# Two-layer attention block with FiLM: a permuted order of calls at the layer change

## The chip, the cores and the metric

One core of one Trainium2 chip runs the kernel. The metric is the device time of one execution in microseconds, from the first to the last work of the core; lower is better. Three runs of the kernel before are shown, and one more execution was recorded by the profiler.

## The reference, cut to what matters

The input x has 32 tiles of 128 tokens by 512 features. Two layers run over each tile, with the weights and masks of their own; a third input, cond, gives a scale and a shift per tile (FiLM).

```python
def layer(x, cond, mask, heads):            # heads: 16 in layer 0, 8 in layer 1
    xn = layernorm(x) * norm_scale + norm_bias
    q, k, v = xn @ Wq + bq, xn @ Wk + bk, xn @ Wv + bv
    k, v = masked(k, mask), masked(v, mask)
    q = softmax(q, over the features of a head)
    k = softmax(k, over the tokens)
    att = k.T @ v                           # per head
    y = q @ att
    scale, shift = split(silu(cond) @ film_W + film_b)
    h = silu(layernorm(y) * (1 + scale) + shift)
    return x + h @ Wo + bo
x = layer(x, cond, mask0, 16); x = layer(x, cond, mask1, 8)
```

All is float32. Each of the four large products is made as three products of split operands (high part times high part, high times low, low times high).

## The kernel before, in words

**Tiles and steps.** A tile is one batch entry (128 x 512). Tiles 0 to 31 belong to layer 0, tiles 32 to 63 are the same rows of X again in layer 1, and step s computes the keys, values and queries of tile s. The kernel is a software pipeline over 64 steps, written out by hand: each engine has a block with a list of calls, and in the steady part one function `step(s)` that lists the calls of one step. Engines meet only at semaphores: a call waits for the counts of its inputs and of the readers of what it overwrites, and raises a count of its own. There is no planner at run time; the order of the calls on each engine is the order of the work. An engine that waits lets nothing of its list pass.

**What a tile goes through.** Tiles of x are turned in pairs g (tiles 2g and 2g+1). VectorE: `stat_x` (mean and variance), GpSimd: `root_x`, ScalarE: `norm_x`, VectorE: `turn_x` (transpose in blocks of 32 by 32), SyncE: `write_x`, `read_x` (through a buffer in HBM, which finishes the transpose), ScalarE: `x_turned` (scale and bias, and the high part XH), GpSimd: `x_low` (the low part XL). TensorE: `keys` (24 matmuls of 256 columns), `values` and `queries` (12 matmuls of 512 columns each). The keys go on by VectorE `keys` (mask, maximum), ScalarE `exp_k`, VectorE `key_sums`, GpSimd `normalise_keys`, VectorE `turn_keys`, and in pairs by SyncE `write_keys` and `place_keys` into EK. The values go by VectorE `values` and ScalarE `values`. The queries go by VectorE `queries`, GpSimd `queries`, VectorE `turn_queries`, then SyncE `write_qy` and `read_qy` into QT, and ScalarE `exp_q`. TensorE: `attention(j)` (32 small matmuls on EK and VV), ScalarE: `heads(j)` (copies the result to ATT), TensorE: `mix(j)` (8 matmuls on EQ and ATT). Then VectorE `mixed`, GpSimd `root_y`, ScalarE `norm_y`, VectorE `turn_y`, again `write_qy` and `read_qy` (q of tile s-1 and y of tile s-3 travel in one transfer, so `exp_q(j)` needs `read_qy(j+1)` and `film(o)` needs `read_qy(o+3)`), ScalarE `film` (four pieces and a tanh), VectorE `h_mul`, ScalarE `h_high`, GpSimd `h_low`, TensorE `output` (12 matmuls of 512 columns), VectorE `add_x`. GpSimd's `add_bo` adds the output bias to X ahead of that.

**Lines.** `split_low` is at 308, `load_second` at 316, the calls of SyncE at 362 to 431, of GpSimd at 573 to 645, of ScalarE at 768 to 893, of TensorE at 1081 to 1205 (all matmuls of the large products have line 1091, attention 1171, mix 1187), of VectorE at 1394 to 1561.

**Buffers that bind the order.** XS, QS, QT, XT, KT, EK, XF0, H, HH and HL exist once; XH, XL, SK and the HBM buffers twice; VV three times. PSUM has one bank each for keys, values, queries and outputs, so `keys(i)` on TensorE waits for VectorE's `keys(i-1)`, and likewise for the others; `attention(j)` waits for `heads(j-1)`:

```python
eng.wait_ge(ld_ek[g % 2], placed(g))   # attention(j), g = j // 2
eng.wait_ge(act_v, j + 1)
eng.wait_ge(act_att, j)
eng.wait_ge(pe_att, j + 1)             # heads(j)
eng.wait_ge(pe_y, j)
```

**The layer change.** Steps 31 to 36 are written out separately on every engine (SyncE 500 to 541, GpSimd 699 to 748, ScalarE 977 to 1046, TensorE 1318 to 1353, VectorE 1737 to 1820), because the four weights of layer 1 come in there. Weight w (4 to 7: k, v, q, o) is loaded into the one buffer STAGE in four chunks by `load_second(eng, w, [c])`, each of which waits until the same chunk of weight w-1 has been split. ScalarE's `split_high(w, [c])` makes the high part and waits until the last product of layer 0 with the old weight is done; VectorE or GpSimd makes the low part by `split_low(eng, w, [c])`. The first product of layer 1 with a weight waits for its chunks one by one:

```python
for c in range(C):
    if fresh is not None:
        eng.wait_ge(low_w[fresh][c], 1)
```

The calls of `load_second_bias` fetch the three bias rows of layer 1. The film weights are loaded in halves behind `write_qy` in even steps up to 20, in `step` of SyncE.

Of the kernel before, what the change touches and what calls it, by code (L numbers as in the profile page):

```python
# [44 lines left out]
def build_blocks(nc, x, cond, mask0, mask1, weights, film_w, vec_rows, bias_rows, out):  # L45
# [21 lines left out]
    with ctx:  # L67
# [273 lines left out]
        def _(eng):  # L341
# [160 lines left out]
            write_qy(31)  # L502
            load_second(eng, 5, [1])
            load_second(eng, 5, [0])
            load_second(eng, 5, [2])
            load_second(eng, 5, [3])
            read_qy(31)
            read_x(17)
            write_keys(15)
            load_second_bias(0, dve_v)  # L510
            load_second(eng, 6, [0])
            load_second(eng, 6, [1])
            load_second(eng, 6, [2])
            load_second(eng, 6, [3])
            place_keys(15)
            load_second_bias(1, dve_q)
            write_qy(32)
            read_qy(32)
            masks_at(32)
            write_keys(16)  # L520
            write_qy(33)
            read_qy(33)
            place_keys(16)
            write_x(18)
            read_x(18)
            write_qy(34)
            read_qy(34)
            masks_at(34)
            load_second(eng, 7, [0])
            load_second(eng, 7, [1])  # L530
            load_second(eng, 7, [2])
            load_second(eng, 7, [3])
            write_x(19)
            write_qy(35)
            read_x(19)
            read_qy(35)
            write_keys(17)
# [18 lines left out]
        def _(eng):  # L556
# [143 lines left out]
            root_y(28)  # L700
            split_low(eng, 4, [1])
            h_low(27)
            x_low(33)
            normalise_keys(31)
            root_x(36)
            mask_of_keys(16)
            queries(31)
            root_y(29)
            h_low(28)
            split_low(eng, 6, [1])  # L710
            split_low(eng, 6, [3])
            x_low(34)
            normalise_keys(32)
            root_x(37)
            normalise_keys(33)
            queries(32)
            root_y(30)
            h_low(29)
            x_low(35)
            root_x(38)  # L720
            mask_of_keys(17)
            queries(33)
            add_bo(32)
            add_bo(33)
            add_bo(34)
            root_y(31)
            h_low(30)
            x_low(36)
            normalise_keys(34)
            root_x(39)  # L730
            queries(34)
            add_bo(35)
            root_y(32)
            h_low(31)
            x_low(37)
            normalise_keys(35)
            root_x(40)
            mask_of_keys(18)
            queries(35)
            add_bo(36)  # L740
            root_y(33)
            split_low(eng, 7, [1])
            split_low(eng, 7, [3])
            h_low(32)
            x_low(38)
            normalise_keys(36)
            root_x(41)
            queries(36)
# [18 lines left out]
        def _(eng):  # L767
# [210 lines left out]
            film(27)  # L978
            norm_y(28)
            exp_q(29)  # L980
            split_high(4, [0])
            split_high(4, [1])
            h_high(27)
            split_high(4, [2])
            split_high(4, [3])
            x_turned(33)
            exp_k(31)
            heads(29)
            split_high(5, [0])
            split_high(5, [1])  # L990
            split_high(5, [2])
            split_high(5, [3])
            film(28)
            values(31)
            h_high(28)
            norm_y(29)
            split_high(6, [0])
            split_high(6, [1])
            split_high(6, [2])
            split_high(6, [3])  # L1000
            exp_q(30)
            norm_x(36)
            x_turned(34)
            exp_k(32)
            heads(30)
            values(32)
            exp_k(33)
            film(29)
            h_high(29)
            norm_y(30)  # L1010
            exp_q(31)
            x_turned(35)
            heads(31)
            norm_x(37)
            values(33)
            film(30)
            h_high(30)
            norm_x(38)
            norm_y(31)
            x_turned(36)  # L1020
            exp_k(34)
            exp_q(32)
            heads(32)
            values(34)
            norm_x(39)
            film(31)
            norm_y(32)
            x_turned(37)
            h_high(31)
            exp_k(35)  # L1030
            exp_q(33)
            heads(33)
            values(35)
            split_high(7, [0])
            split_high(7, [1])
            split_high(7, [2])
            split_high(7, [3])
            norm_x(40)
            film(32)
            norm_y(33)  # L1040
            x_turned(38)
            h_high(32)
            exp_k(36)
            exp_q(34)
            heads(34)
# [31 lines left out]
        def _(eng):  # L1077
# [254 lines left out]
            queries(33)  # L1332
            attention(31)
            output(29)
            mix(31)
            keys(34)
            values(34)
            queries(34)
# [9 lines left out]
            keys(36)  # L1348
            values(36)
            queries(36)  # L1350
# [544 lines left out]
```

## Time and profile before

| what | value |
|---|---|
| median of three runs | 878.02 us (877.77 to 879.38) |
| profiled execution | 877.97 us, span of its instructions 876.2 us |
| mean granted clock of TensorE | 0.994 |
| busy in the span: TensorE, VectorE, ScalarE, GpSimd | 843.5, 679.9, 607.6, 549.5 us |
| transfers | 169.81 MB, 194 GB/s over the span |
| chain that ended last | TensorE 84%, DMA 6%, VectorE 4% |

The span runs from the first to the last instruction; the execution's own time has 1.8 us more around it. All times in the views below are counted from the start of the span. Busy time of TensorE counts matmuls whatever their clock, so a slow clock hides in it; the granted clock stands beside it as a share of full speed.

### The profile page before, as it was taken

What the parts mean: (1) busy time and instruction counts of PE and PEld (TensorE: products, weight loads), DVE (VectorE), ACT (ScalarE), POOL (GpSimd) and SP (SyncE); (2) the same over time, 40 slices, a digit from 0 to 9 for tenths busy, and PEclk for the clock granted to TensorE, in tenths of its full rate; (3) what the DMA queues carried; (4) which work ended last, traced back from release to release, by engine and by line L of the source; (5) the groups of instructions that cost most, each with busy time, mean ns of one, the idle gap of its engine ahead of it and who ended that gap; (6) DMA issues with size and microseconds to landing.
All of it is one profiled execution on the core that took longest, in us unless ns stands there. A gap on an engine that the chain in (4) does not pass through costs nothing.

```text
span 876.2 us, 19904 instructions
## 1 busy us (share of the span) xinstructions
PE 843.5 (96%) x6581; PEld 715.2 (82%) x6581; DVE 679.9 (78%) x1352; ACT 607.6 (69%) x1441; POOL 549.5 (63%) x741
## 2 busy tenths in 40 slices
PE   4989999999999999999978999999999999999997
PEld 4768888888888888888867888888888888888885
DVE  5987777778778778877977887787788788777765
ACT  5566777676777677677775866776776777677564
POOL 2475765765766766676657667667656766765541
PEclk9999999999999999999999999999999999999999
DMA  9875766776766665556754656556666655656431
GB/s 315 292 205 172 221 206 188 223 213 196 222 199 204 205 216 186 167 176 192 211 175 151 217 174 200 183 182 196 186 193 199 200 177 178 195 192 198 150 134 61
DMA packets 115549, 169.81 MB, mean 194 GB/s; under 512 B 11871, under 2 KB 84695, under 8 KB 115447
## 3 DMA queue, kind: packets, MB, share of 16 engines
q1 hardware_dynamic: 114656, 167.56, 60.9%
q8 instruction: 53, 0.87, 0.4%
q10 hardware_dynamic: 790, 0.98, 0.4%
q14 instruction: 50, 0.40, 0.2%
HBM read 95.61 MB, written 72.88 MB: 192 GB/s over the span
## 4 chain that ended last, share of the span: by engine, by line
PE 84%; DMA 6%; DVE 4%; issue 2%; ACT 2%; SPq 2%; POOL 0%; ACTq 0%; DVEq 0%
PE PS L1091 74%; PE PS L1187 6%; PE PS L1171 3%; DMA QT<-qy_turned 1%; DMA x_turned<-XS 1%; DMA X<-in_x 1%; DMA qy_turned<-QS 1%; SPq L405 1%; DMA k_turned<-KT 0%; PE PS L1233 0%; SPq L420 0%; DVE WL_k L313 0%; DMA EK<-k_turned 0%; DMA XT<-x_turned 0%; SPq L380 0%
## 5 line engine op out<-in xcount | busy, mean ns | idle before, releaser
L635 POOL TENSOR_TENSOR HL<-H,HH 128x512 fp32r<-128x512 f32 x60 | 78.3, 1305 | 186.6 <-ACT HH L855 186.4
L822 ACT ACTIVATE Z<-QT,FC,FA 128x128 f32<-128x128 f32 x240 | 99.1, 484 | 100.4 <-DMA QT<-qy_turned 100.4
L1091 PE MATMUL PS<-XH,WH_k 128*128 128x256 f32 x512 | 152.0, 297 | 2.6 <-DVE XL L1448 2.5
L1091 PE MATMUL PS<-XH,WL_k 128*128 128x256 f32 x512 | 146.5, 286 | 0.0
L1091 PE MATMUL PS<-XL,WH_k 128*128 128x256 f32 x512 | 146.5, 286 | 0.0
L1091 PE MATMUL PS<-WH_o,HH 128*128 128x512 f32 x248 | 104.2, 420 | 6.6 <-issue 6.4
L892 ACT ACTIVATE XN<-X,NBX,RSX 128x512 f32<-128x512 f32 x60 | 48.8, 813 | 79.2 <-POOL NBX L584 79.2
L1091 PEld LDWEIGHTS PS<-XH,WH_k 128*128 128x128 f32 x512 | 99.9, 195 | 4.2 <-issue 4.1
L784 ACT ACTIVATE SK<-SK,KN 128x128 f32<-128x128 f32 x256 | 98.9, 387 | 5.9 <-DVE KN L1466 5.9
L1091 PE MATMUL PS<-WH_q,XH 128*128 128x512 f32 x256 | 101.4, 396 | 0.3 <-DVE SQ L1493 0.3
L1091 PE MATMUL PS<-WH_v,XH 128*128 128x512 f32 x256 | 100.6, 393 | 0.0
L1091 PE MATMUL PS<-WL_q,XH 128*128 128x512 f32 x256 | 100.4, 392 | 0.0
L1091 PE MATMUL PS<-WL_v,XH 128*128 128x512 f32 x256 | 100.3, 392 | 0.0
L1091 PE MATMUL PS<-WH_q,XL 128*128 128x512 f32 x256 | 100.2, 391 | 0.0
L1091 PEld LDWEIGHTS PS<-XL,WH_k 128*128 128x128 f32 x512 | 100.0, 195 | 0.0
L1091 PEld LDWEIGHTS PS<-XH,WL_k 128*128 128x128 f32 x512 | 99.7, 195 | 0.0
L1091 PE MATMUL PS<-WH_v,XL 128*128 128x512 f32 x256 | 99.6, 389 | 0.0
L1091 PE MATMUL PS<-WL_o,HH 128*128 128x512 f32 x248 | 98.1, 396 | 0.0
L1091 PE MATMUL PS<-WH_o,HL 128*128 128x512 f32 x248 | 98.0, 395 | 0.0
L622 POOL TENSOR_TENSOR XL<-XF,XH 128x512 fp32r<-128x512 f32 x60 | 77.7, 1295 | 9.1 <-ACT XH L881 8.9
L606 POOL TENSOR_TENSOR X<-X,BB 128x512 f32<-128x512 f32 x64 | 82.8, 1296 | 0.4
L1561 DVE TENSOR_TENSOR X<-PS,X 128x512 f32<-128x512 f32 x64 | 44.2, 690 | 46.0 <-PE PS L1091 45.9
(155 smaller groups left out, 2111.4 us busy)
## 6 DMA issues: line engine op xcount, KB each, us to landing
qy_turned<-QS SPq DMA_DIRECT2D x60, 512.0 KB, 2.9
QT<-qy_turned SPq DMA_DIRECT2D x240, 128.0 KB, 3.0
k_turned<-KT SPq DMA_DIRECT2D x32, 512.0 KB, 4.1
EK<-k_turned SPq DMA_DIRECT2D x128, 128.0 KB, 2.8
x_turned<-XS SPq DMA_DIRECT2D x30, 512.0 KB, 2.8
XT<-x_turned SPq DMA_DIRECT2D x120, 128.0 KB, 3.5
out_x<-X SPq DMA_DIRECT2D x32, 256.0 KB, 3.4
X<-in_x SPq DMA_DIRECT2D x11, 512.0 KB, 4.9
```

The lines of the kernel that those rows point to most:

```text
L405: eng.dma_start(QT[32 * fq:32 * fq + 32, :, 0:n, :, :].rearrange("p q h c n -> p q (h c n)"), src[fq])\
L606: eng.tensor_tensor(X[:, b, :], X[:, b, :], BB[:, 2, :], ALU.add).then_inc(pool_bo, 1)
L622: eng.tensor_tensor(XL[g % 2][:, dst, :], XF0[:, :, :], XH[g % 2][:, dst, :].bitcast(F32), ALU.subtract).then_inc(pool_xl, 1)
L635: eng.tensor_tensor(hl_of(o), h_of(o), hh_of(o).bitcast(F32), ALU.subtract).then_inc(pool_hl, 1)
L784: e = eng.activation(SK[:, p, a, :], SK[:, p, a, :], ACT.Exp, bias=KN[:, p, t, cc:cc + 1], accum_out=SE[:, p, a:a + 1])
L822: z = eng.activation(z_of(o)[:, c * P:c * P + P].rearrange("p (q n) -> p q n", q=Q), src, ACT.Identity, bias=FC[l][:, c, b:b + 1], scale=F ...
L892: eng.activation(XN[:, t, :], X[:, n % B, :], ACT.Identity, bias=NBX[:, r:r + 1], scale=RSX[:, r:r + 1]).then_inc(act_xn, 1)
L1091: mm = eng.matmul(dst, left[a](c), right[b](c), start=(c == 0 and a + b == 0), stop=(c == C - 1 and a == 1))
L1171: mm = eng.matmul(PS[f:f + 32, B_ATT, c * P + a:c * P + a + w], vs if l == 0 else ks, ks if l == 0 else vs, start=True, stop=True, tile_po ...
L1187: mm = eng.matmul(bank(B_Y + c // 2, (c % 2) * W, W), EQ[:, c * P:c * P + P], ATT[:, c // 2, (c % 2) * W:(c % 2 + 1) * W], start=True, sto ...
L1561: eng.tensor_tensor(X[:, b, :], PS[:, bank_out(o), :], X[:, b, :], ALU.add).then_inc(dve_x, 1)
```

## The change

Only the order of calls in steps 31 to 36 changes, on all five engines. Every list holds the same calls before and after, so each instruction and each transfer is issued once as before, with the same waits and sizes. Out of their places move 22 calls of TensorE's list, 73 of VectorE's, 64 of ScalarE's, 40 of GpSimd's and 34 of SyncE's (counted as positions at which the lists differ). The loading of the film halves is in the steady steps and is left as it is. On TensorE:

```diff
@@ -1318,36 +1318,36 @@
 keys(31)
 values(31)
 queries(31)
+keys(32)
 attention(29)
+keys(33)
+mix(29)
 output(27)
-mix(29)
-keys(32)
-keys(33)
 values(32)
 output(28)
 attention(30)
+attention(31)
+mix(30)
 queries(32)
-mix(30)
 values(33)
 queries(33)
-attention(31)
-output(29)
 mix(31)
 keys(34)
+queries(34)
 values(34)
-queries(34)
 attention(32)
+output(29)
+mix(32)
+queries(35)
 output(30)
-mix(32)
 keys(35)
+attention(33)
 values(35)
-queries(35)
-attention(33)
 output(31)
 mix(33)
 keys(36)
+queries(36)
 values(36)
-queries(36)
 attention(34)
 output(32)
 mix(34)
```

On the other engines the order after the change is this (the order before is in the functions above, at the lines named).

SyncE, lines 500 to 541:

```python
load_second(eng,5,[0]); load_second(eng,5,[1]); load_second(eng,5,[2]); write_qy(31); load_second(eng,5,[3]);
load_second(eng,6,[0]); read_qy(31); write_keys(15); load_second(eng,6,[1]); write_x(17);
load_second(eng,6,[2]); place_keys(15); load_second_bias(0, dve_v); load_second_bias(1, dve_q);
load_second(eng,6,[3]); load_second_bias(2, pool_bo); read_x(17); write_qy(32); read_qy(32); masks_at(32);
load_second(eng,7,[0]); write_keys(16); write_qy(33); masks_at(34); load_second(eng,7,[1]); read_qy(33);
place_keys(16); write_qy(34); write_x(18); read_qy(34); load_second(eng,7,[2]); load_second(eng,7,[3]);
read_x(18); write_qy(35); read_qy(35); write_x(19); write_keys(17); read_x(19); place_keys(17); write_qy(36);
read_qy(36); masks_at(36)
```

GpSimd, lines 699 to 748:

```python
add_bo(31); root_y(28); root_x(36); split_low(eng,4,[1]); x_low(33); normalise_keys(31); mask_of_keys(16);
queries(31); h_low(27); h_low(28); root_y(29); normalise_keys(32); root_x(37); split_low(eng,6,[1]);
split_low(eng,6,[3]); normalise_keys(33); root_y(30); x_low(34); queries(32); add_bo(32); x_low(35);
root_x(38); root_x(39); mask_of_keys(17); root_x(40); root_y(31); queries(33); h_low(29); add_bo(33);
add_bo(34); add_bo(35); queries(34); h_low(30); root_y(32); add_bo(36); h_low(31); x_low(36);
normalise_keys(34); x_low(37); mask_of_keys(18); normalise_keys(35); queries(35); root_y(33); h_low(32);
split_low(eng,7,[1]); root_x(41); split_low(eng,7,[3]); normalise_keys(36); queries(36); x_low(38)
```

ScalarE, lines 977 to 1046:

```python
norm_x(35); x_turned(33); split_high(4,[0]); split_high(4,[1]); norm_y(28); split_high(4,[2]);
split_high(4,[3]); film(27); split_high(5,[0]); exp_k(31); exp_q(29); values(31); h_high(27);
split_high(5,[1]); split_high(5,[2]); heads(29); split_high(5,[3]); split_high(6,[0]); film(28); exp_q(30);
h_high(28); exp_k(32); exp_k(33); split_high(6,[1]); norm_y(29); heads(30); split_high(6,[2]);
split_high(6,[3]); heads(31); x_turned(34); values(32); x_turned(35); norm_y(30); exp_q(31); norm_x(36);
film(29); norm_x(37); norm_y(31); h_high(29); exp_q(32); film(30); norm_x(38); heads(32); norm_x(39);
h_high(30); values(33); exp_k(34); film(31); exp_q(33); norm_y(32); h_high(31); x_turned(36); x_turned(37);
exp_k(35); heads(33); split_high(7,[0]); norm_x(40); split_high(7,[1]); split_high(7,[2]); film(32);
exp_q(34); norm_y(33); h_high(32); values(34); split_high(7,[3]); exp_k(36); heads(34); x_turned(38);
values(35); values(36)
```

VectorE, lines 1737 to 1820:

```python
stat_x(36); mixed(28); stat_x(37); stat_x(38); turn_queries(30); split_low(eng,4,[0]); turn_x(35); turn_y(28);
split_low(eng,4,[2]); keys(31); split_low(eng,4,[3]); values(31); split_low(eng,5,[0]); h_mul(27);
key_sums(31); add_x(26); queries(31); split_low(eng,5,[1]); turn_keys(31); keys(32); split_low(eng,5,[2]);
split_low(eng,5,[3]); mixed(29); h_mul(28); add_x(27); keys(33); key_sums(32); split_low(eng,6,[0]);
stat_x(39); stat_x(40); key_sums(33); turn_queries(31); turn_y(29); split_low(eng,6,[2]); mixed(30);
values(32); queries(32); turn_keys(32); turn_keys(33); turn_queries(32); turn_y(30); add_x(28); values(33);
mixed(31); queries(33); h_mul(29); turn_x(36); second_ones(); keys(34); turn_queries(33); turn_y(31);
queries(34); turn_x(37); h_mul(30); add_x(29); mixed(32); turn_x(38); turn_x(39); key_sums(34);
turn_queries(34); h_mul(31); turn_y(32); add_x(30); values(34); queries(35); keys(35); values(35); stat_x(41);
key_sums(35); turn_keys(34); turn_keys(35); mixed(33); add_x(31); split_low(eng,7,[2]); turn_queries(35);
h_mul(32); split_low(eng,7,[0]); turn_y(33); keys(36); queries(36); turn_x(40); key_sums(36); values(36);
turn_keys(36)
```

## Rows read from the trace of the kernel before

**Rows 1.** The page: busy time and share of the span of each engine

```profile
PE 843.5 (96%) x6581; PEld 715.2 (82%) x6581; DVE 679.9 (78%) x1352; ACT 607.6 (69%) x1441; POOL 549.5 (63%) x741
```

**Rows 2.** Windows: length, busy us by engine, granted clock, DMA share, GB/s

```profile
400.00:450.00 50.00, 45.62 (x368) 38.80 (x368) 41.30 (x74) 36.03 (x82) 33.20 (x41) 0.97 0.72 208
450.00:500.00 50.00, 45.68 (x330) 38.85 (x330) 38.53 (x76) 34.59 (x80) 34.25 (x45) 0.97 0.55 175
...
700.00:800.00 100.00, 99.97 (x782) 85.13 (x781) 78.64 (x156) 73.04 (x175) 65.61 (x88) 1.00 0.58 188
...
445.00:450.00 5.00, 4.51 (x43) 3.63 (x44) 2.48 (x7) 4.08 (x14) 2.92 (x4) 0.66 0.43 139
```

**Rows 3.** The chain, 400 to 540: start us, us, what (mix 27, 28, 34, 35)

```profile
403.40 0.90 PE PS L1187 x8
...
416.02 0.91 PE PS L1187 x8
...
505.80 0.90 PE PS L1187 x8
...
518.62 0.90 PE PS L1187 x8
```

**Rows 4.** Timeline of TensorE: start, us, line, tiles, shape, count, idle before and releaser

```profile
425.18 0.46 PE L1171 MATMUL PS<-EK,VV 128*32 128x32 f32 x32
...
439.78 0.47 PE L1091 MATMUL PS<-WH_o,HH 128*128 128x512 f32 x1 [1.44 <-issue]
...
445.49 0.46 PE L1171 MATMUL PS<-EK,VV 128*32 128x32 f32 x32 [2.67 <-DMA EK<-k_turned]
...
450.33 1.06 PE L1187 MATMUL PS<-ATT,EQ 128*128 128x132 f32 x8
...
477.48 2.10 PE L1187 MATMUL PS<-ATT,EQ 128*128 128x132 f32 x8 [3.22 <-ACT EQ L802]
```

**Rows 5.** Timeline of SyncE's queue, the issue of place_keys(15)

```profile
437.40 1.75 SPq L420 DMA_DIRECT2D EK<-k_turned  x4
```

**Rows 6.** The chain, 400 to 540: transfers of the q and y rounds

```profile
440.60 6.44 DMA qy_turned<-QS
...
448.37 4.24 DMA QT<-qy_turned
...
457.86 2.59 DMA qy_turned<-QS
```

**Rows 7.** Timeline of ScalarE: heads(29), and the first piece of x_turned(36)

```profile
427.29 0.57 ACT L841 ACTIVATE ATT<-PS 128x512 f32<-128x512 f32 x1
...
473.09 1.10 ACT L874 ACTIVATE XF<-XT,VC 128x256 f32<-128x256 f32 x2 [2.05 <-DMA XT<-x_turned]
```

**Rows 8.** VectorE's groups, 415 to 510: shapes, count | busy us, mean ns | idle before

```profile
L313 DVE TENSOR_TENSOR WL_k<-STAGE,WH_k 128x512 fp32r<-128x512 f32 x3 | 5.1, 1764 | 0.0
...
L1400 DVE BATCH_NORM_STATS2 BNX<-X 128x6 f32<-128x512 f32 x6 | 4.1, 678 | 0.0
...
L1464 DVE TENSOR_TENSOR KB<-KM,VC 128x4 f32<-128x4 f32 x6 | 3.1, 521 | 0.2
...
L313 DVE TENSOR_TENSOR WL_q<-STAGE,WH_q 128x512 fp32r<-128x512 f32 x2 | 1.3, 671 | 1.5 <-ACT WH_q L774 1.5
```

**Rows 9.** Timeline of VectorE: turn_x(35), keys(31), h_mul(27); mixed(29), h_mul(28)

```profile
418.80 0.68 DVE L1422 STREAM_TRANSPOSE XS<-XN 128x512 f32<-128x512 f32 x1
...
420.00 0.65 DVE L1460 TENSOR_TENSOR SK<-PS,MB 128x512 f32<-128x512 f32 x1
...
421.69 0.68 DVE L1547 SCALAR_TENSOR_TENSOR H<-H,Z 128x512 f32<-128x512 f32 x1
...
434.73 0.24 DVE L1527 RECIPROCAL RQ<-PS 128x16 f32<-128x16 f32 x1
...
436.56 0.66 DVE L1547 SCALAR_TENSOR_TENSOR H<-H,Z 128x512 f32<-128x512 f32 x1
```

**Rows 10.** The page: GpSimd's h_low, mean ns of one

```profile
L635 POOL TENSOR_TENSOR HL<-H,HH 128x512 fp32r<-128x512 f32 x60 | 78.3, 1305 | 186.6 <-ACT HH L855 186.4
```

More of the change, by code:

```diff
@@ L499, in _ @@
                 step(s)
-            write_x(17)
-            load_second_bias(2, pool_bo)
[L502 to L507, printed above, removed]
-            read_x(17)
[L509 to L516, printed above, removed]
+            load_second(eng, 5, [0])
+            load_second(eng, 5, [1])
+            load_second(eng, 5, [2])
+            write_qy(31)
+            load_second(eng, 5, [3])
+            load_second(eng, 6, [0])
+            read_qy(31)
+            write_keys(15)
+            load_second(eng, 6, [1])
+            write_x(17)
+            load_second(eng, 6, [2])
+            place_keys(15)
+            load_second_bias(0, dve_v)
+            load_second_bias(1, dve_q)
+            load_second(eng, 6, [3])
+            load_second_bias(2, pool_bo)
+            read_x(17)
             write_qy(32)
@@ L977, in _ @@
             norm_x(35)
-            film(27)
-            norm_y(28)
-            exp_q(29)
+            x_turned(33)
             split_high(4, [0])
             split_high(4, [1])
-            h_high(27)
+            norm_y(28)
             split_high(4, [2])
             split_high(4, [3])
-            x_turned(33)
+            film(27)
+            split_high(5, [0])
             exp_k(31)
-            heads(29)
-            split_high(5, [0])
+            exp_q(29)
+            values(31)
@@ L990, in _ @@
+            h_high(27)
             split_high(5, [1])
             split_high(5, [2])
+            heads(29)
             split_high(5, [3])
+            split_high(6, [0])
             film(28)
-            values(31)
+            exp_q(30)
             h_high(28)
+            exp_k(32)
+            exp_k(33)
+            split_high(6, [1])
             norm_y(29)
-            split_high(6, [0])
-            split_high(6, [1])
+            heads(30)
             split_high(6, [2])
             split_high(6, [3])
-            exp_q(30)
@@ L1002, in _ @@
-            norm_x(36)
+            heads(31)
             x_turned(34)
-            exp_k(32)
-            heads(30)
             values(32)
-            exp_k(33)
-            film(29)
-            h_high(29)
+            x_turned(35)
             norm_y(30)
             exp_q(31)
-            x_turned(35)
-            heads(31)
+            norm_x(36)
+            film(29)
             norm_x(37)
-            values(33)
[L1016 to L1019, printed above, removed]
@@ L1020, in _ @@
-            x_turned(36)
[L1021 to L1027, printed above, removed]
+            norm_y(31)
+            h_high(29)
+            exp_q(32)
+            film(30)
+            norm_x(38)
+            heads(32)
+            norm_x(39)
+            h_high(30)
+            values(33)
+            exp_k(34)
+            film(31)
+            exp_q(33)
+            norm_y(32)
+            h_high(31)
@@ L1028, in _ @@
+            x_turned(36)
             x_turned(37)
-            h_high(31)
             exp_k(35)
-            exp_q(33)
             heads(33)
-            values(35)
             split_high(7, [0])
+            norm_x(40)
             split_high(7, [1])
             split_high(7, [2])
+            film(32)
+            exp_q(34)
+            norm_y(33)
+            h_high(32)
+            values(34)
             split_high(7, [3])
-            norm_x(40)
-            film(32)
-            norm_y(33)
+            exp_k(36)
@@ L1041, in _ @@
+            heads(34)
             x_turned(38)
[L1042 to L1045, printed above, removed]
+            values(35)
             values(36)
```

158 lines of the change are left out of this document (79 added, 79 removed).

## Prediction, made before the changed kernel was seen to run

> **What bounds the kernel now.** I began with the page: TensorE is busy in 843.5 of 876.2 us, no other engine in more than 680 [rows 1]. So TensorE is the bound, and what can be won is its idle time. The windows say where that lies: in 100 us late in layer 1 it is busy 99.97 us, but at the layer change it misses 4.38 us of 400 to 450 and 4.32 of 450 to 500 [rows 2]. In one of these stretches the granted clock is 0.66 (between the levels 1.2 and 2.4 GHz), so some time is lost while TensorE counts as busy [rows 2].
>
> The whole price comes from the chain, which passes through every mix. Two mixes of layer 0 lie 416.02 - 403.40 = 12.62 us apart, two of layer 1 518.62 - 505.80 = 12.82 [rows 3]. From mix(28) at 416.02 to mix(34) at 505.80 there are six steps, three with attention of each layer: 3 x 12.62 + 3 x 12.82 = 76.3 us if nothing waits. They take 89.8. **13.5 us** is the most that this change can give.
>
> The timeline of TensorE and the chain's transfers tell who takes them. Output(28) comes after 1.44 us of idle; attention(30) after 2.67, waiting for EK [rows 4]. Then from attention(30) at 445.49 to mix(30) at 450.33 pass 4.84 us where a full clock needs 3.2: 1.6 us to the clock, after a stretch with two holes. Mix(32) waits 3.22 us for exp_q(32), and its eight matmuls take 2.10 us, against some 0.9 in the chain of other steps [rows 3, 4]. The rest, 13.5 - 1.4 - 2.7 - 1.6 - 3.2 - 1.2 = 3.4, is in short holes and the slow matmuls behind mix(32). Why EK is late: place_keys(15) is issued at 437.40 behind four weight chunks, and attention(30) starts 8.1 us later [rows 5]. The write of QS at 440.60 takes 6.44 us to land, a like one at 457.86 takes 2.59; its read takes 4.24 [rows 6]. Why exp_q(32) is late: on ScalarE it stands behind x_turned(36) and exp_k(34), and x_turned(36) starts only at 473.09, after 2.05 us of waiting for read_x(18) [rows 7], which exp_q(32) has no need of.
>
> **The change, engine by engine.** It adds and removes no instruction and no transfer: each engine issues the same calls in another order, with the same waits. Direct cost zero; the price is in who waits for whom. I walked the new order by hand with durations of the trace, from 416.02, where both kernels are still alike.
>
> *Weight splits and keys(32).* New: keys(32) stands directly behind queries(31), free at 425.18 [rows 4], instead of behind attention, output and mix. It needs the split chunks of weight 4 and VectorE's keys(31). The first of the two transposes ahead of VectorE's keys(31) began at 418.80, right behind mixed(28), and keys(31) itself at 420.00, so a transpose is worth 0.6. From 418.8 the new order has two stat_x (0.68 and an aggregate: 0.8 each), three transposes (turn_queries, turn_x, turn_y: 0.62 each), two splits (0.65 each) and keys(31), which takes 421.69 - 420.00 = 1.69 [rows 8, 9]: 1.6 + 1.9 + 1.3 + 1.7 = 6.5, thus 425.3. Split 4[3] follows at 425.9 and is needed only by the last quarter of a product. One collision with GpSimd (below) would add 1.1. Loss: between 0.1 and 1.3, I take **0.7**, the middle, since one of the two splits faces GpSimd's own.
>
> *Keys(33), mix(29), output(27).* Keys(33) covers heads(29), which is good. Output(27) needs h_low(27), now behind root_x(36), the split, x_low(33), normalise_keys(31), the mask and queries(31) on GpSimd: my walk has it 0.1 us after mix(29). Between 0 and one h_low of 1.3 [rows 10]; I take **0.1**, as all that stands before it was ready early.
>
> *Output(28).* Film(28) needs read_qy(31), which SyncE may issue only after split 4[3], split 5[0] and exp_q(29); h_mul(28) waits on VectorE for mixed(29) behind four splits; then h_high and h_low. TensorE has values(32) to do meanwhile. Between 0 and the present 1.44; **0.5** by the walk.
>
> *Attention(30), attention(31), mix(30).* Place_keys(15) now has only two chunks and a write ahead of it instead of four chunks, and its keys are turned at about 431.3. A write of 4 us and a placing of 5, between the transfers of [rows 6], put EK at 440 to 441, and attention(30) wants it at 441.6. But attention(31) now stands directly behind attention(30) and needs heads(30), which reads what attention(30) wrote: a bubble of 0.57 [rows 7] and two handovers, **0.7**, that the old order did not have. In return attention(31) need not be fetched in later.
>
> *Queries(32), values(33).* Values(33) needs values(32) of VectorE, behind split 6[2] and mixed(30) (436.56 - 434.73 = 1.83 [rows 9]): **0.3**, between 0 and 1.1.
>
> *Steps 34 to 36.* Queries(34) goes ahead of values(34), output(29) goes behind attention(32), output(30) behind queries(35). So h_low(29) and h_low(30) gain three to six us of cover. On ScalarE, exp_q(32) stands ahead of both x_turned(36) and exp_k(34), so the 3.22 us wait and its slow clock go. Exp_q(33) and exp_q(34) come 7 us or more ahead of their mixes. Cost 0 in the walk. This cover is work of TensorE itself; without it the 3.22 would be back. What is late next are places with less than 0.8 us to spare: exp_q(31) for mix(31) (0.5), x_low(35) for keys(34) (0.7), EK for attention(32) and (34) (0.5 each), h_low(29) and (30) (0.6, 0.8), split 7[3] for output(32) (0.3). For these seven I add **2.0**, between 0 and 7 x 0.6 = 4.2; nearest to the low end, since a slip shifts all later work on other engines too and a second place pays only the difference.
>
> *The queues.* SyncE's waits are strict: write_qy(33) now waits behind write_keys(16) and a chunk of weight 7; read_qy(34) behind write_x(18), which waits for turn_x(37). Both are in the walk; the latter's cover is 4 us. Masks_at(34) and two chunks of weight 7 move up, to the calm behind step 32. GpSimd comes out of step 36 some 4 us later relative to mix(34) than now (x_low(38) behind mix(34), not ahead of it), and keys(38) wants x_low(39) 3 us after it can be ready: hidden. The film halves are loaded in earlier steps, unchanged.
>
> **Sum.** 0.7 + 0.1 + 0.5 + 0.7 + 0.3 + 2.0 = 4.3 us lost of 13.5: a gain of 9.2. The profiled execution took 877.97 (span 876.2 and 1.8 around it), so 868.8; the median, 878.02, stands 0.05 above it, which I neglect. After step 36 TensorE is saturated, so a gain there stays a gain at the end. From the ends of the terms: lost 0 + 0.1 + 0 + 0.7 + 0 + 0 to 1.3 + 1.3 + 1.4 + 0.7 + 1.1 + 4.2, or 0.8 to 10.0, times of 865.3 to 874.5, all at one end only together.
>
> **One row against the change: the collisions.** A split of weight 4 on VectorE takes 1764 ns, one of weight 6 takes 671; the sum KB, with both inputs in SBUF, four elements wide, takes 521 on average [rows 8]. The long ones ran while GpSimd worked on wide tiles. The Trainium skill (SBUF — State Buffer, section Who interferes with whom) says that a VectorE operation with two SBUF inputs and a GpSimd operation that reads SBUF lock each other out for a whole instruction. The trace agrees for the splits of weight 4. The new order packs splits, h_mul and keys on VectorE against h_low, mask and queries on GpSimd between 421 and 437, where TensorE hangs on VectorE.
>
> **The rivals.** *A, collisions everywhere.* The five splits that gate (4[0], 4[2], 5[1] to 5[3]) each lose 1764 - 671 = 1.1: 5.5 us in place of the 0.7 and some of the thin places: 868.8 + 5.5 - 1.7 = **872.6**. For: the three of weight 4 all lost it. Against: those of weight 5 did not, on average. 0.17.
> *B, transfers as crowded as now, and the clock with them.* EK takes 8.1 us from its issue again [rows 5]: issued about 435.5, it lands at 443.6, 2.0 after attention(30) wants it, and the clock falls again for 1.6: 868.8 + 3.6 = **872.4**. Against: two of the four chunks now come after it. 0.12. The Trainium skill (TensorE: Matmul & The Clock Gate, HAM oscillation) says too that waits for DMA take the clock down; the trace agrees at 445 to 450 [rows 2], and rival B has its price from rows.
> *C, slower: the round of q and y becomes the bound.* Rounds 31, 32 and 33 (write, read, then exp_q and film) each gate TensorE with at most 1.0, 0.5 and 0.6 us to spare. If each write takes 6.44 instead of 2.59 [rows 6], 3 x 3.85 - 2.1 = 9.5 are lost beside the 2.3 of the sum's first terms and 3.2 of clock: 15.0 against 13.5, **879.5**. It decides from about 3.4 us of excess (13.5 - 2.3 - 3.2 + 2.1, by three) in each of the three. Against: only one write in this stretch took that long, and the crowd of chunks ahead of it is spread now. 0.07.
> *D, nothing gained: the idle time only moves.* GpSimd's lag of 4 us after step 36, if its slack of 3 is not there, makes each following step wait until the old phase is restored: up to the whole 9.2, **878**. Against: GpSimd is busy in 549.5 of 876.2 us [rows 1]. 0.05.
> The forecast itself: 0.59.
>
> **How the numbers follow.** Likeliest: 868.8. The range 865.8 to 873.9 takes in the forecast's bounds nearly whole and A and B with a us of excess; outside are C, D and the far ends of the others, under 0.2. A measurement of this kernel can tell 0.2% (1.8 us) from no change. Faster by more: forecast, A and B, 0.88. Within: D, 0.05. Slower: C, 0.07.
>
> **What would show it.** The windows 400 to 450 and 450 to 500 should show TensorE busy 47 to 49 us each, with no granted clock under 0.9 in any 5 us. Mix(34) should come near 496.6. The waits of TensorE should name no EQ, and EK for under 1 us. ScalarE should do exp_q(32) ahead of x_turned(36). Right for A: splits of weights 4 and 5 with a mean over 1200 ns. Wrong altogether: a wait of over 2 us on QT or EK, or one on XL after 500.

## The result, and the profile after

| | before | after |
|---|---|---|
| median of 6 runs each, same chip | 878.31 us (877.55 to 881.51) | 872.59 us (871.42 to 874.24) |
| ratio, 95% interval | | 0.9927 (0.9911 to 0.9944) |
| profiled execution, span | 877.97, 876.2 us | 871.58, 869.8 us |
| mean granted clock | 0.994 | 0.994 |

The change makes the kernel 5.7 us faster, where 9.2 were forecast. The page's busy line of after answers to [rows 1]: each engine is busy for as long as before, within 3 us, in a shorter span.

```profile
PE 843.4 (97%) x6581; PEld 715.4 (82%) x6581; DVE 677.0 (78%) x1352; ACT 606.4 (70%) x1441; POOL 548.5 (63%) x741
```

The windows of after, with the columns of [rows 2]:

```profile
400.00:450.00 50.00, 48.33 (x419) 40.85 (x419) 43.43 (x88) 38.29 (x93) 35.39 (x47) 1.00 0.69 207
450.00:500.00 50.00, 48.00 (x340) 40.58 (x339) 39.42 (x75) 36.38 (x83) 37.02 (x46) 0.97 0.67 205
...
465.00:470.00 5.00, 4.42 (x43) 3.55 (x44) 1.50 (x3) 3.07 (x6) 4.16 (x4) 0.72 0.83 284
```

TensorE has gained 2.71 and 2.32 us of busy time in the two stretches of the layer change. One slow stretch is left, now at 465 to 470. The chain of after, 400 to 540 (start us, us, what), gives the price by the mixes of [rows 3] (mix 28 and 34):

```profile
417.13 0.91 PE PS L1187 x8
...
454.30 3.48 DMA qy_turned<-QS
...
461.79 3.75 DMA EK<-k_turned
465.58 0.65 PE PS L1171 x32
...
499.28 0.90 PE PS L1187 x8
```

From mix(28) at 417.13 to mix(34) at 499.28 pass 82.15 us. Before it was 89.8, and 76.3 without any wait. So 5.8 us are still lost, and 7.6 of 13.5 are won. The waits of TensorE from 400 to 540 (releaser: us in total, times, longest us) say where they are:

```profile
PE PS L1171 <- DMA EK<-k_turned: 2.0, 1, 2.0
PE PS L1171 <- ACT ATT L841: 0.9, 1, 0.9
PE PS L1091 <- DVE KN L1466: 0.7, 1, 0.7
```

The wait on EQ of [rows 4] is gone. The timeline of TensorE shows the same three idle times at keys(32), attention(31) and attention(32), and a fourth loss that no wait shows:

```profile
427.12 0.35 PE L1091 MATMUL PS<-XH,WH_k 128*128 128x256 f32 x1 [0.75 <-DVE KN L1466]
...
444.38 0.46 PE L1171 MATMUL PS<-EK,VV 128*32 128x32 f32 x32 [0.93 <-ACT ATT L841]
...
465.58 0.65 PE L1171 MATMUL PS<-VV,EK 128*32 128x64 f32 x32 [2.00 <-DMA EK<-k_turned]
...
466.51 0.39 PE L1091 MATMUL PS<-WL_o,HH 128*128 128x512 f32 x1
...
468.07 0.63 PE L1091 MATMUL PS<-WH_o,HH 128*128 128x512 f32 x1
...
470.61 1.06 PE L1187 MATMUL PS<-ATT,EQ 128*128 128x132 f32 x8
```

Inside output(29) a matmul takes first 0.39 and then 0.63 us: the clock has gone down behind the hole, toward the lower of its two levels (0.72 of 2.4 GHz over the 5 us). From attention(32) at 465.58 to mix(32) at 470.61 pass 5.03 us. A variant shown below (the round of y earlier) has the same calls there at a full clock: 465.50 to 468.99, 3.49 us. The clock cost 1.5.

At attention(30), where before waited 2.67 us for EK, TensorE's matmuls show no wait. But it was close. The weight load ahead of its matmuls (engine PEld) still waits:

```profile
442.99 0.35 PEld L1171 LDWEIGHTS PS<-EK,VV 128*32 128x32 f32 x32 [0.37 <-DMA EK<-k_turned]
```

Place_keys(15) was issued at 436.38, 6.6 us ahead of that.

Why EK is late stands in the timeline of SyncE (start and length of the issue):

```profile
451.79 0.43 SPq L411 DMA_DIRECT2D k_turned<-KT  x1
454.30 0.33 SPq L390 DMA_DIRECT2D qy_turned<-QS  x1
...
457.80 2.53 SPq L405 DMA_DIRECT2D QT<-qy_turned  x4
460.42 1.80 SPq L420 DMA_DIRECT2D EK<-k_turned  x4
```

The keys that place_keys(16) fetches were written by the issue of 451.79, and that write landed 4.7 us later, near 456.5. But place_keys(16) stands behind read_qy(33), which waits for write_qy(33), issued at 454.30 and landed at 457.78 (the chain's 3.48 us). So place_keys(16) goes out at 460.42, lands at 465.54, and attention(32) starts at 465.58. Write_qy(33) in turn waits for turn_y(30) (453.51), which ScalarE's norm_y(30) sets (452.68). That stands in line behind x_turned(35) (451.02), which waits for GpSimd's x_low(34) (449.62 to 450.92). Two things end just ahead of x_low(34): x_turned(34) of ScalarE (447.50 to 449.25) and GpSimd's own root_y(30) (to 449.53), which stands ahead of it in the list. X_turned(34) waited for read_x(17), issued at 440.15 and landed at 447.48, 7.3 us later.

### The profile page after: what moved, and what is told of

It reads as the page before. It is cut to its first block, busy times and chain, and to the rows that moved or that the text cites. A ratio compares the mean times of both kernels' runs of the same rounds, so it can differ in the third digit from the quotient of the medians.

```text
span 869.8 us, 19904 instructions
## 1 busy us (share of the span) xinstructions
PE 843.4 (97%) x6581; PEld 715.4 (82%) x6581; DVE 677.0 (78%) x1352; ACT 606.4 (70%) x1441; POOL 548.5 (63%) x741
## 4 chain that ended last, share of the span: by engine, by line
PE 81%; DMA 8%; DVE 3%; ACT 2%; SPq 2%; issue 2%; POOL 1%; DVEq 0%; ACTq 0%; POOLq 0%
PE PS L1091 71%; PE PS L1187 6%; PE PS L1171 3%; DMA X<-in_x 2%; DMA QT<-qy_turned 2%; DMA k_turned<-KT 2%; SPq L405 1%; DMA qy_turned<-QS 1%; DMA EK<-k_turned 1%; DMA XT<-x_turned 1%; SPq L420 1%; ACT XF L874 1%; PE PS L1233 0%; PE PS L1243 0%; ACT YN L791 0%
```

## The experiments

Below, "28 to 34" is the time from mix(28) to mix(34) in the profiled execution (89.8 before, 82.15 after). The ratio is always to the kernel before on the same chip. Three chips were used for the experiments: the first for the repeat and the next three runs (before had a median of 878.92 us there), the second for weight 7 late, the stat_x, the round of y and the three mends together (880.10), the third for the last four (879.65). The changed kernel was run again on the first alone, so a later order is compared with it across chips. Between the times of two executions there is a shift as well: mix(28) begins at 415.0 to 417.4 over the 14 traces of this study. And from mix(34) to mix(58) they take 307.7 to 309.6 us, so that a difference of a us between 28 and 34 need not show in the median.

**The same kernel again,** without any edit, on the chip of the next three.

> The changed kernel once more, beside the other orders of this call. 872.6 by its runs so far; all theories expect 871.5 to 874, with attention(32) some 2 us late on EK and a slow output(29) behind it.

It took 871.16 us, 0.9921 (0.9902 to 0.9939) of before, with 82.9 us from mix(28) to mix(34). The wait on EK is 1.8 us, the clock from 465 to 470 is 0.73. The size of the gain and both halves of the loss at attention(32) are the kernel's and not one execution's.

**Place_keys(16) ahead of read_qy(33)** on SyncE.

```diff
-read_qy(33)
 place_keys(16)
+read_qy(33)
```

> SyncE issues place_keys(16) ahead of read_qy(33) instead of behind it. Theory 1 (the queue's own order: the keys landed in HBM at 456.5 but place_keys(16) was issued at 460.4, behind the wait for the write of q and y): EK lands near 461.5, the wait of attention(32) (2.0) and the slow clock behind it (1.6) go, 3.6 us less than the changed kernel, about 869.0. Theory 2 (the transfers are crowded, so EK lands late wherever it is issued): within 1 us of the changed kernel. Theory 3 (collisions of VectorE and GpSimd took the gain): no change.

871.94 us, 0.9927 (0.9910 to 0.9944), 28 to 34 82.4 us; the 869.0 of the first theory did not come. The timeline of SyncE, and then those of TensorE and ScalarE:

```profile
457.06 1.75 SPq L420 DMA_DIRECT2D EK<-k_turned  x4
458.92 2.72 SPq L405 DMA_DIRECT2D QT<-qy_turned  x4
```

```profile
454.48 1.17 PE L1187 MATMUL PS<-ATT,EQ 128*128 128x132 f32 x8 [1.09 <-ACT EQ L802]
...
463.95 0.65 PE L1171 MATMUL PS<-VV,EK 128*32 128x64 f32 x32
...
469.35 1.14 PE L1187 MATMUL PS<-ATT,EQ 128*128 128x132 f32 x8 [1.75 <-issue]
```

```profile
465.23 0.63 ACT L802 ACTIVATE EQ<-QT 128x512 f32<-128x512 f32 x1 [3.25 <-DMA QT<-qy_turned]
```

Attention(32) no longer waits, and the clock stays full. So the place of the loss is right: the queue's order made EK late. But the time is the same. The read of q and y is now issued 1.1 us later, ScalarE waits 3.25 us for it, exp_q(32), film(30) and heads(32) follow late, and mix(32) waits 1.75 us. Mix(31) loses another 1.09. Which of two transfers goes first moves the wait; both cannot be early in a queue with that much ahead of them.

**Chunk 3 of weight 6 and read_x(17) ahead of the three bias rows,** to take away the first cause of the late norm_y(30).

```diff
 place_keys(15)
+load_second(eng, 6, [3])
+read_x(17)
 load_second_bias(0, dve_v)
 load_second_bias(1, dve_q)
-load_second(eng, 6, [3])
 load_second_bias(2, pool_bo)
-read_x(17)
```

> Weight chunk 6[3] and read_x(17) go ahead of the three bias rows. Theory 1 with its root one step earlier (x_turned(34) waits for read_x(17), so norm_y(30), turn_y(30), write_qy(33), read_qy(33) and place_keys(16) are all late): x_turned(34) starts 1 to 2 us earlier and place_keys(16) with it, so the wait for EK halves: 1 to 3 us less than the changed kernel. If read_x(17) is only one of several equals, under 0.5.

872.15 us, 0.9921 (0.9897 to 0.9946); 28 to 34 81.2 us. The read landed near 445.7 and x_turned(34) began at 446.29, 1.2 us earlier than in after. The wait on EK stayed at 1.89. X_low(34) came only 0.2 us earlier, as GpSimd does it behind its own root_y(30); its timeline:

```profile
449.06 0.27 POOL L594 TENSOR_SCALAR NBY<-MVY,RSY 128x1 f32<-128x1 f32 x1
449.41 1.30 POOL L622 TENSOR_TENSOR XL<-XF,XH 128x512 fp32r<-128x512 f32 x1
```

So x_turned(35) (450.81) and norm_y(30) (452.47) were 0.2 us earlier too, and no more. That cause, taken alone, is refuted. The clock stayed full behind this hole, which is about what 28 to 34 is shorter (0.9 to 1.7 us). The median does not show it: from mix(34) to mix(58) this execution took 309.63 us, 1.7 more than after.

**SyncE's list as in before,** with the new order on the four other engines (its 34 places, listed ahead of the prediction, go back to the order of before).

> SyncE's order of before, the other engines as in the changed kernel. Theory 1: the order of the queue matters a lot; place_keys(16) stands behind read_qy(33) here too and masks_at(34) and weight 7 come later: 0 to 3 us slower than the changed kernel. Theory 2 (crowding): the chunks of weight 6 are again all ahead of place_keys(15), EK is late for attention(30) as in the kernel before, 2 to 4 us slower, near 875. If the gain was all in the compute engines: within 1 us of the changed kernel.

891.06 us, 1.0142 (1.0121 to 1.0163); 28 to 34 102.1 us. Waits of TensorE, 400 to 540:

```profile
PE PS L1091 <- POOL HL L635: 7.0, 1, 7.0
PE PS L1091 <- DVE VV L1505: 6.9, 1, 6.9
PE PS L1187 <- issue: 3.7, 1, 3.7
```

None of the theories allowed for that much: the worst had 2 to 4 us more than after, and it is 20. The orders of the five engines belong together. With SyncE's left behind, the same change costs 12 us instead of giving 6. The releasers named are compute engines, though only the order of transfers differs from after: they are late themselves. Part of the loss is the clock, 0.51 from 450 to 455 and 0.50 from 495 to 500, behind the two holes of 7 us.

**Place_keys(16) ahead, and two chunks of weight 7 and masks_at(34) behind read_qy(34).**

```diff
-load_second(eng, 7, [0])
 write_keys(16)
 write_qy(33)
-masks_at(34)
-load_second(eng, 7, [1])
-read_qy(33)
 place_keys(16)
+read_qy(33)
 write_qy(34)
 write_x(18)
 read_qy(34)
+masks_at(34)
+load_second(eng, 7, [0])
+load_second(eng, 7, [1])
 load_second(eng, 7, [2])
```

> Place_keys(16) ahead of read_qy(33) as before, and masks_at(34) with weight chunks 7[0] and 7[1] moved back behind read_qy(34). With place_keys(16) alone ahead, the wait went from EK at attention(32) to EQ at mix(31) and mix(32). If those are late because the transfers of steps 32 and 33 are crowded by the chunks and the mask (theory 2), read_qy(33) lands 2 us or more earlier, mix(32) does not wait, and the time is 868.5 to 870. If it is the chain of q and y before the write that is late (theory 1b), read_qy(33) lands within 1 us of where it did and the time stays at 871 to 872.

875.83 us, 0.9951 (0.9933 to 0.9968); 28 to 34 85.1 us. Timeline of ScalarE, then of TensorE:

```profile
480.54 1.09 ACT L874 ACTIVATE XF<-XT,VC 128x256 f32<-128x256 f32 x2 [2.90 <-DMA XT<-x_turned]
```

```profile
487.64 1.14 PE L1187 MATMUL PS<-ATT,EQ 128*128 128x132 f32 x8 [2.74 <-issue]
```

Up to mix(32) the order does what it was meant to: that mix no longer waits and comes 51.9 us after mix(28), against 53.8 with place_keys(16) ahead alone. But all four chunks now stand in one block ahead of read_x(18), which lands near 480.5. X_turned(36) waits for it, and behind that stand heads(33) and film(32). Mix(33) waits 2.74 us. The chunks have to go somewhere; ahead of read_x(18) is the wrong place.

**The four stat_x of the change put later** on VectorE: 37 and 38 where 39 and 40 stood, 39 behind turn_keys(33), 40 behind h_mul(29).

```diff
-stat_x(37)
-stat_x(38)
 turn_queries(30)
...
-stat_x(39)
-stat_x(40)
+stat_x(37)
+stat_x(38)
...
 turn_keys(33)
+stat_x(39)
...
 h_mul(29)
+stat_x(40)
```

> Stat_x(37) to (40) move behind keys(33) and behind turn_keys(33) on VectorE. The sum's term for keys(32) (0.7) is that VectorE's chain ahead of the splits of weight 4 is too long: the 0.75 of idle time before keys(32) goes, keys(33) of VectorE ends 1.8 us earlier. If the layer's second half is bound by its own chain, the time falls by 0 to 0.8 us only; if all is one chain, by up to 1.5.

871.56 us, 0.9907 (0.9885 to 0.9930); 28 to 34 81.5 us. It can't be told apart from after. Keys(32) still waits 0.68 us. (The wait for EK at attention(32) is 1.19 here, with a full clock behind it, and attention(34) waits 0.69 for its own.) Timeline of VectorE:

```profile
422.10 0.69 DVE L313 TENSOR_TENSOR WL_k<-STAGE,WH_k 128x512 fp32r<-128x512 f32 x1 [1.00 <-ACT WH_k L774]
...
423.93 1.57 DVE L313 TENSOR_TENSOR WL_k<-STAGE,WH_k 128x512 fp32r<-128x512 f32 x1
425.42 0.68 DVE L1460 TENSOR_TENSOR SK<-PS,MB 128x512 f32<-128x512 f32 x1
```

With 1.8 us of work less, VectorE reaches the first split of weight 4 before ScalarE's high part is there, and waits 1.00. The second split takes 1.57 us instead of the 0.69 of the first, beside GpSimd's work. Keys(31) of VectorE (425.42) is no earlier than in after (425.06); counted from mix(28), which began 0.43 us later here, it comes at the same time within 0.1. My chain of durations on VectorE was therefore only one of two that meet here.

**The round of y earlier:** norm_y(30) ahead of x_turned(35) on ScalarE, and root_x(40) behind root_y(31) and queries(33) on GpSimd.

```diff
+norm_y(30)
 x_turned(35)
-norm_y(30)
...
-root_x(40)
 root_y(31)
 queries(33)
+root_x(40)
```

> Norm_y(30) goes ahead of x_turned(35) on ScalarE, which stood idle for 1.1 us there, and root_x(40) behind queries(33) on GpSimd, so root_y(31) comes 1.6 us earlier. Theory 1b (write_qy(33) waits for turn_y(30), and all behind it on SyncE's queue with it): write_qy(33) is issued about 1 us earlier, EK for attention(32) lands about 1 us earlier, and 1 us of the 2.0 of idle time there goes, and perhaps the slow clock (1.6): 1 to 2.6 us under the changed kernel. Theory 2 (crowding): 0 to 0.5 us.

871.04 us, 0.9895 (0.9877 to 0.9913); 28 to 34 81.9 us. SyncE, then TensorE:

```profile
453.37 0.33 SPq L390 DMA_DIRECT2D qy_turned<-QS  x1
...
457.95 2.76 SPq L405 DMA_DIRECT2D QT<-qy_turned  x4
460.81 2.04 SPq L420 DMA_DIRECT2D EK<-k_turned  x4
```

```profile
465.50 0.65 PE L1171 MATMUL PS<-VV,EK 128*32 128x64 f32 x32 [2.14 <-DMA EK<-k_turned]
...
468.99 1.06 PE L1187 MATMUL PS<-ATT,EQ 128*128 128x132 f32 x8
```

Norm_y(30) is 2.6 us earlier (450.04), but the write only 0.9, as turn_y(30) now stands right behind turn_queries(32), which waits for GpSimd:

```profile
451.99 0.71 DVE L1432 STREAM_TRANSPOSE QS<-SQ 128x512 f32<-128x512 f32 x1 [1.21 <-POOL SQ L613]
```

(Mix(28) began 1.4 us earlier in this execution, so even the 0.9 may not be the edit's.) And the write lands no earlier (457.94 against 457.78): it takes 4.6 us now, 3.5 in after. So an earlier norm_y(30) doesn't bring EK forward; what keeps it back is when the write lands, and the order behind it. That other transfers hold the write up was not tried by itself, but the traces speak for it. In the six that have chunk 0 of weight 7 ahead of this write, mask and chunk 1 right behind it, and its issue at 453.4 to 454.9, it takes 3.5 to 4.7 us; in the four in which chunks and mask come later, 2.8 to 3.7. In one more, with the chunk ahead but the write issued at 457.63, it takes 2.8. The hole of 2.14 us draws no slow clock here. The ratio is lower than that of after by about as much as the intervals are wide, but the medians of the changed kernel on the first chip (871.16) and of this one (871.04) are the same, and so is 28 to 34: a gain is not shown.

**All three mends together:** weight 7 late with place_keys(16) ahead, the stat_x late, the round of y earlier.

> All three edits at once: place_keys(16) ahead, weight 7 and the mask later, norm_y(30) and root_y(31) earlier, four stat_x later. If the losses left are what the changed kernel's waits say (0.75 at keys(32), 2.0 at attention(32), 1.6 of clock behind it), they go and only heads(30) (0.9) and handovers stay: 4 us under the changed kernel, 867.5 to 868.5. If each edit only moves the wait to the next transfer, 870 to 872.

874.38 us, 0.9947 (0.9929 to 0.9965); 28 to 34 84.0 us, above both of the ranges expected. Mix(32) comes 51.1 us after mix(28) (53.6 in after), then mix(33) waits 2.50 for the late read_x(18), as in the run of weight 7 late. Two of the mends do not make up for that one.

**One part of the change alone, on the kernel before:** exp_q(32) and heads(32) ahead of x_turned(36) and exp_k(34) on ScalarE.

```diff
+exp_q(32)
+heads(32)
 x_turned(36)
 exp_k(34)
-exp_q(32)
-heads(32)
```

> The kernel before with one part of the change alone: exp_q(32) and heads(32) ahead of x_turned(36) on ScalarE. If the 3.22 us wait of mix(32) and the slow clock behind it (1.0 in mix(32), 0.6 in keys(35)) come from this order alone, the time is 4 to 4.9 us under the kernel before. If the step is bound by the x round too (x_turned(36) and (37) now 1.2 us later, keys(36) waits for them), 1 to 3 us under it.

879.50 us, 1.0005 (0.9988 to 1.0022); 28 to 34 89.3 us. Timeline of TensorE:

```profile
472.53 1.06 PE L1187 MATMUL PS<-ATT,EQ 128*128 128x132 f32 x8
...
485.98 0.77 PE L1091 MATMUL PS<-WH_o,HH 128*128 128x512 f32 x1 [3.47 <-issue]
```

The 3.22 us wait of mix(32) in [rows 4] goes, and its eight matmuls take 1.06 us instead of 2.10. All of it comes back at output(31), which waits 3.47, with a clock of 0.50 from 485 to 490 behind it. Both of the gains expected (4 to 4.9 us, or 1 to 3) failed to come. The largest single wait of the kernel before is worth nothing by itself: what stands behind exp_q(32) on ScalarE is about as late as it was. Counted from mix(28), x_turned(36) comes 0.8 us earlier and h_high(31), which output(31) needs, 1.1.

**SyncE's queue mended:** place_keys(16) ahead of read_qy(33), two chunks of weight 7 and the mask behind it, and read_x(18) ahead of the other two chunks.

```diff
-load_second(eng, 7, [0])
 write_keys(16)
 write_qy(33)
-masks_at(34)
-load_second(eng, 7, [1])
-read_qy(33)
 place_keys(16)
+read_qy(33)
+load_second(eng, 7, [0])
+load_second(eng, 7, [1])
+masks_at(34)
 write_qy(34)
 write_x(18)
 read_qy(34)
+read_x(18)
 load_second(eng, 7, [2])
 load_second(eng, 7, [3])
-read_x(18)
```

> The changed kernel with another order on SyncE alone: place_keys(16) ahead of read_qy(33), chunks 7[0], 7[1] and masks_at(34) behind read_qy(33), read_x(18) ahead of 7[2] and 7[3]. When all four chunks went ahead of read_x(18), x_turned(36) waited 2.9 us for it and mix(33) 2.7; with read_x(18) ahead of two of them that wait should be gone. Theory of the crowded queue (each transfer waits behind those issued before it): neither attention(32) nor mix(33) waits, mix(32) under 1 us: 1 to 3 us under the changed kernel, a ratio of 0.989 to 0.991. If the chain of q and y alone sets the time: 0.992 to 0.994.

869.66 us, 0.9883 (0.9870 to 0.9896); 28 to 34 80.8 us. SyncE, TensorE, and the window in which after had its slow clock:

```profile
454.14 0.32 SPq L390 DMA_DIRECT2D qy_turned<-QS  x1
455.91 3.48 SPq L420 DMA_DIRECT2D EK<-k_turned  x4
459.50 1.98 SPq L405 DMA_DIRECT2D QT<-qy_turned  x4
```

```profile
463.63 0.65 PE L1171 MATMUL PS<-VV,EK 128*32 128x64 f32 x32
...
468.59 1.14 PE L1187 MATMUL PS<-ATT,EQ 128*128 128x132 f32 x8 [1.31 <-issue]
```

```profile
465.00:470.00 5.00, 3.69 (x20) 2.89 (x19) 2.49 (x4) 4.97 (x11) 3.44 (x4) 1.00 0.85 300
```

Place_keys(16) goes out at 455.91, 4.5 us earlier than in after. The wait on EK and the slow clock are gone; what is left at mix(32) is 1.31 us. This version beats the kernel before on its own chip, and its interval lies below that of after (0.9911 to 0.9944) and of after again (0.9902 to 0.9939), which were not measured beside it. How much it is worth over the changed kernel is less certain: 3.3 to 3.9 us by the ratios, 1.5 to 2.9 by the medians, 1.3 to 2.1 by 28 to 34. In this order chunks 0 and 1 of weight 7 and a mask have moved too, so the gain is not that of place_keys(16) alone.

**The same with the mends on ScalarE, VectorE and GpSimd.**

> That order of SyncE with norm_y(30) and root_y(31) earlier and four stat_x later. Left are heads(30) (0.9), keys(32) (0.7) and handovers: a loss of about 3 us against the 5.8 of the changed kernel, a ratio to the kernel before of 0.987 to 0.989. If the stations do not add up, not below 0.990.

871.40 us, 0.9894 (0.9879 to 0.9910); 28 to 34 80.5 us. Not to be told apart from the queue's mend alone; in microseconds its median is that of the changed kernel on the first chip. Keys(32) keeps its 0.7, attention(31) its 0.93 and mix(32) 1.26.

**Attention(31) behind queries(32)** on TensorE, to take away the bubble (a short idle time of TensorE) that the change brought.

```diff
 attention(30)
+queries(32)
 attention(31)
 mix(30)
-queries(32)
```

> The changed kernel with queries(32) between attention(30) and attention(31) on TensorE. The bubble of heads(30) (0.93) goes, but queries(32) then comes 2.3 us earlier and needs split 6[1], done at 445.5, and split 6[3], done at 447.2: TensorE waits there instead, 1 to 2 us. Expected: between 0.5 us faster and 1.5 us slower than the changed kernel. If it is 0.9 faster, the weights were not late next.

876.51 us, 0.9960 (0.9946 to 0.9974); 28 to 34 86.2 us. Waits of TensorE, 400 to 540:

```profile
PE PS L1091 <- DVE VV L1505: 3.5, 2, 2.6
PE PS L1091 <- POOL WL_q L313: 1.2, 1, 1.2
```

The bubble of 0.93 goes; queries(32) now comes before GpSimd has split its weight (1.2), and mixed(30) and values(32) on VectorE come later for values(33) (2.6), with a clock of 0.69 from 450 to 455 behind that hole. From mix(28) to mix(34) it is 4.1 us slower than after, where at most 1.5 were expected. The bubble is the cheaper of the two.

## Why the prediction was right, and where it was not

**Direction and place: right.** TensorE is the bound, the loss was 13.5 us between mix(28) and mix(34), and what is won there stays: from mix(34) to mix(58) before takes 307.75 us, after 307.91. Rival D (idle only moves) falls for the whole change, by these two numbers. It holds for the single part tried alone, exp_q(32).

**Keys(32), 0.7 forecast:** 0.75 measured. **Heads(30), 0.7:** 0.93. **Output(27), 0.1, output(28), 0.5, and values(33), 0.3:** no wait of theirs shows in after; the repeat has 0.45 at output(28), and so, within 0.13, have four of the variants. Cover on TensorE for the outputs and exp_q(32) ahead of x_turned(36) did what the walk said.

**The step that failed** is the term for thin places, 2.0 for seven, and in it "EK for attention(32) and (34) (0.5 each)". Attention(32) alone cost 2.0 of waiting and 1.5 of clock, 3.5 us. Two statements fell with it: no granted clock under 0.9 (0.72 at 465 to 470), and EK for less than 1 us. The sign for "wrong altogether", a wait of over 2 us on EK, was just not passed: the profile has 2.00. What was wrong in the walk is the queue ahead of place_keys(16). Place_keys(16) waits there behind read_qy(33); the write of q and y took 3.5 us to land (2.59 in the last of [rows 6]), the issue of its read 2.53 (1.7 in quiet steps), and EK another 5.1 from its own issue. Behind two strict waits in one queue such differences add up. The run with place_keys(16) ahead shows the place: wait and slow clock go. But there the time did not fall, as the wait went to q and y. The mended queue, in which q and y wait less too, is worth 1.3 to 3.9 us by the measures given above.

By terms, the loss is 0.75 + 0.93 + 2.0 + 1.5 = 5.2 and 0.6 of small rest, 5.8 in all, against 4.3 forecast. The thin places were 1.5 us dearer than their 2.0 by attention(32) alone, 2.1 with the rest; the 0.9 forecast for the outputs and values(33), of which nothing came in this execution, hid part of that, which was luck. So 1.5 us of the miss are the sum's. The other 2.3 of the difference between 868.8 and 872.59 come from elsewhere. Mix(28) itself began 1.1 us later in this execution than in that of before. The median lies 1.0 above the profiled execution. The last 0.2 are in the steps after mix(34) and in the rounding of the terms.

One price in the account of before was misread. The prediction set the 2.10 us of mix(32)'s matmuls in the timeline beside 0.9 in the chain. In the timeline a mix at full clock takes 1.06, so the slow clock cost 1.0 there and not 1.2; the total of 13.5 does not hang on it.

**The rivals.** *A, collisions:* refuted for weights 4 and 5. The groups of VectorE in after, 415 to 510 (count | busy us, mean ns):

```profile
L313 DVE TENSOR_TENSOR WL_v<-STAGE,WH_v 128x512 fp32r<-128x512 f32 x4 | 2.7, 684 | 0.0
...
L313 DVE TENSOR_TENSOR WL_k<-STAGE,WH_k 128x512 fp32r<-128x512 f32 x3 | 2.2, 735 | 0.0
...
L313 DVE TENSOR_TENSOR WL_q<-STAGE,WH_q 128x512 fp32r<-128x512 f32 x2 | 2.0, 1000 | 0.4 <-ACT WH_q L774 0.4
```

Weight 4's splits fall from the 1764 of [rows 8] to 735. One of the two of weight 6 took 1.32 us, and no wait of TensorE names it. The time of A, 872.6, was nearly the measured one, but by another way. *B, transfers as crowded as now, with the clock:* its price came, one pair of steps later, and mostly by another way. At attention(30) no matmul waits on EK, though it came 6.6 us after its issue, between the forecast (440 to 441) and B's 8.1 us; at attention(32) there is 2.0 plus 1.5, against the 2.0 plus 1.6 in B's price. But there EK took 5.1 us from its issue. It was late because it was issued at 460.42, behind two waits. Crowding has a share in that, the 3.5 us of the write. (B's argument "two of the four chunks now come after it" was wrong as well: in the new list only chunk 3 of weight 6 stands behind place_keys(15); chunk 0 went ahead of write_keys(15).) The queue should have been walked for every place_keys of the stretch, not only for the one that was late before. *C, the round of q and y as the bound:* no; no wait on EQ or film shows on TensorE in after. In the run with place_keys(16) ahead it appears, with 1.09 and 1.75 us.

**The statements for the profile:** the windows (47 to 49 each: 48.33 and 48.00) and the absence of EQ held. Mix(34) was to come near 496.6 and came at 499.28: 1.1 for the later start, 1.5 for the region.

**What stays open:** what sets the last 0.7 at keys(32). Two chains meet there within half a us, VectorE's own work and the high part of weight 4 from ScalarE, and the runs show only that removing one doesn't help.

## What to carry to other kernels

In a queue whose waits are strict, ask of each transfer not when its data is ready but what waits ahead of it, and give every transfer under load a range up to the longest duration that the trace shows, not the shortest alone. A term for thin places should be made for each place alone and include the fall of the clock where the place is a wait of TensorE on a transfer. The largest wait of a profile can be worth nothing by itself, as exp_q(32) was here, and still have to go for a consistent order to pay. And an order that helps on four engines can cost more than it gives if the fifth is left as it was, 12 us here. Before the times of two executions are compared, count them from a point where both are still alike.

## What the runs showed of the hardware that was not expected

The fall of the clock does not follow from the length of a hole alone. Behind attention(32)'s hole of 2.00 us (1.8 in the repeat) the granted clock was 0.72 (0.73) from 465 to 470, in both traces of the same kernel. Behind holes of 2.14 and 1.89 us at the same place, in the runs with the y round and read_x(17) earlier, it was 1.00. What else decides is open. Nor is it the kind of wait. Behind output(31)'s 3.47 us in the run of exp_q(32), behind 2.64 us for VectorE in the run with queries(32) ahead, and behind 6.87 us for VectorE in the run with SyncE's old list, the profile names no transfer as the releaser, and the clock was 0.50, 0.69 and 0.50 over the 5 us in which the hole ended. The Trainium skill (TensorE: Matmul & The Clock Gate, HAM oscillation) tells of a kernel in which waits for DMA, of some 3 to 5 us each, took the clock down every time. The waits for DMA here are shorter, and two of these four traces agree and two don't.

The landing of a write did not follow its issue. The write of q and y took 3.48 us when issued at 454.30, and 4.57 when issued 0.93 us earlier in another execution, and landed within 0.16 us of the same moment.
